# One-hots of a counting sort on Trainium2: bfloat16 digits in pairs from SBUF in place of float32 digits against numbers in PSUM

## What is computed

```python
qkv = x @ qkv_w + qkv_b                              # 12500 x 64 @ 64 x 128
s, t = src, dst
qe = q[s] * 8**-0.5 + (edge_attr @ q_rpe_w + q_rpe_b)
ke = k[t] + (edge_attr @ k_rpe_w + k_rpe_b)
ve = v[t] + (edge_attr @ v_rpe_w + v_rpe_b)
compat = einsum('ehd,ehd->eh', qe, ke)               # 4 heads of 8
ex = exp(compat - segment_max(compat, s)[s])
attn = ex / (segment_sum(ex, s)[s] + 1e-16)
out = segment_sum((ve * attn[..., None]).reshape(e, 64), s)
y = layernorm(x + out)
```

## Time and profile before

| | |
|---|---|
| timed executions | 4825.19 us median (4823.5 to 4829.62) |
| profiled execution, its span | 5645.0 us |
| VectorE busy | 4200.5 us, 74% |
| TensorE busy | 3997.8 us, 71%; weight loads 3559.9 us, 63% |
| GpSimd busy | 3570.5 us, 63% |
| ScalarE busy | 2869.3 us, 51% |
| granted TensorE clock | 0.50 from 282 to 5076 us, 0.97 to 0.99 after |
| DMA engines | 34% to 35% in the sort, 83% to 98% after |

### The profile page before, as it was taken

How to read it: one execution, slowest core, us unless ns; L and a number is a source line. 1 busy time by engine, 2 the same in 40 slices (tenths; PEclk the granted TensorE clock), 3 DMA queues, 4 the chain that set the end, 5 groups by cost and what they waited for, 6 DMA issues and landing times. The chain is left out here.

```text
span 5645.0 us, 94294 instructions
## 1 busy us (share of the span) xinstructions
PE 3997.8 (71%) x18783; PEld 3559.9 (63%) x18783; DVE 4200.5 (74%) x18085; ACT 2869.3 (51%) x6600; POOL 3570.5 (63%) x3772
## 2 busy tenths in 40 slices
PE   7777676777776677677666767777776767748886
PEld 6666666666666666666666666666666666637765
DVE  7777777777777777777777777777777777759998
ACT  3555455555555455455545555555555555524555
POOL 2566666666666666666666666666666666647887
PEclk6555555555555555555555555555555555559999
DMA  6333333333333333333333333333333333369996
GB/s 182 106 110 109 109 107 108 106 107 110 107 111 107 107 110 106 105 111 107 108 107 109 109 110 107 105 112 108 104 110 104 113 108 107 107 159 394 371 356 246
DMA packets 379094, 759.55 MB, mean 135 GB/s; under 512 B 143060, under 2 KB 206875, under 8 KB 365883
## 3 DMA queue, kind: packets, MB, share of 16 engines
q1 hardware_dynamic: 255493, 385.24, 23.1%
q0 software_dynamic: 123520, 373.41, 18.4%
HBM read 570.54 MB, written 187.75 MB: 134 GB/s over the span
## 5 line engine op out<-in xcount | busy, mean ns | idle before, releaser
L634 POOL DMA_INDIRECT rec_dram<-recs,place_i x3223 | 3087.9, 958 | 1819.0 <-issue 1634.2
L670 DVE SCALAR_TENSOR_TENSOR matches<-ids_b,src_f,ps_const 128x128 bf16<-128x128 int16 (+3 forms) x3232 | 1643.9, 543 | 543.5 <-issue 524.0
L786 PE MATMUL ps_feat<-w_in,edge_in 51*128 51x128 f32 x6464 | 1688.5, 438 | 31.9 <-issue 31.4
L769 PE MATMUL ps_look<-free_rec,lo_hotT 128*128 128x98 f32 x6464 | 1609.3, 431 | 1.9 <-ACT lo_hotT L812 1.9
L786 PEld LDWEIGHTS ps_feat<-w_in,edge_in 51*128 51x128 f32 x6464 | 1442.7, 325 | 177.6 <-issue 177.0
L769 PEld LDWEIGHTS ps_look<-free_rec,lo_hotT 128*128 128x128 f32 x6464 | 1473.1, 333 | 2.1 <-ACT lo_hotT L812 2.1
L760 PE MATMUL ps_cnt<-hi_hot,lo_hot 128*128 128x98 bf16 x3232 | 406.0, 276 | 1407.8 <-ACT free_rec L824 787.7
L824 ACT ACTIVATE free_rec<-ps_cnt 128x98 f32<-128x98 f32 x808 | 194.7, 241 | 2366.5 <-remote 2242.4
L760 PEld LDWEIGHTS ps_cnt<-hi_hot,lo_hot 128*128 128x128 bf16 x3232 | 238.3, 127 | 1617.9 <-issue 873.9
L679 DVE CUSTOM_DVE_ANT_0 picked<-hi_hot,ps_look 128x98 f32<-128x98 bf16 x3232 | 652.9, 252 | 123.4 <-issue 114.0
L659 DVE TENSOR_TENSOR lo_hot<-lo_f,ps_const 128x512 bf16<-128x512 bf16 (+1 forms) x808 | 549.9, 681 | 39.0 <-issue 39.0
(11 more groups left out here) (187 smaller groups left out, 2282.0 us busy)
## 6 DMA issues: line engine op xcount, KB each, us to landing
ids_b<-id_dram SPq DMA_DIRECT2D x808, 384.0 KB
rec_dram<-recs,place_i POOLq DMA_INDIRECT x3223
edge_in<-in_attr SPq DMA_DIRECT2D x808, 36.0 KB
w_in<-kv_dram SPq DMA_DIRECT2D x808, 12.0 KB
qx_dram<-qx SPq DMA_DIRECT2D x1, 4753.0 KB
kv_dram<-kvt SPq DMA_DIRECT2D x14, 336.0 KB, 3.7
xt<-in_xT SPq DMA_DIRECT2D x14, 224.0 KB, 3.7
origin<-in_dst_tiles SPq DMA_DIRECT2D x1, 1616.0 KB, 9.3
```

What stands on the lines that cost most here:

```text
L634: pool.indirect_dma_start(rec_dram[:, :], bass.IndirectOffsetOnAxis(place_i[j][:, m:m + 1], 0), recs[j][:, m, 0:ROW], None).then_inc(scatt ...
L670: last = dve.scalar_tensor_tensor(matches[j % NS][:, junk:junk + before], ids_b[j][:, 1, 0:before], src_f[:, bass.ds(u * CT + m, 1)], ps_c ...
L769: last = nc.tensor.matmul(ps_look[j % NS][:, m, 0:NB], lo_hotT[j % NS][:, P * m:P * (m + 1)], free_rec[j % 2][:, :], start=True, stop=True)
L786: last = nc.tensor.matmul(ps_feat[j % 2][:, m, :], edge_in[j][0:K_ROWS, tile], w_in[j][0:K_ROWS, :], start=True, stop=True)
```

## The change

The digits `lo_f` and `hi_f` are stored as bfloat16 in place of float32 (both hold whole numbers up to 127). `lo_hot` and `hi_hot` take the layout of the tables stage: two tiles innermost, [pair of tiles, number, tile of the pair]. The numbers 0 to 127, each twice, stand in a bfloat16 tile `number` in SBUF in place of slice 0 of `ps_const` in PSUM. So both inputs of the two comparisons are bfloat16 in SBUF with two adjacent elements innermost. TensorE's products and VectorE's pick read the one-hots with a step of two elements. One constant's transposition on TensorE goes, and a VectorE cast of 128 x 128 becomes one of 128 x 256. No instruction of the loops is added, removed or moved on any engine; the lines below `number` are one number higher than before (L659 becomes L660).

```diff
-        T["lo_f"] = digits.enter_context(nc.sbuf_tensor("lo_f", [P, NT], F32))
-        T["hi_f"] = digits.enter_context(nc.sbuf_tensor("hi_f", [P, NT], F32))
+        T["lo_f"] = digits.enter_context(nc.sbuf_tensor("lo_f", [P, NT], BF16))
+        T["hi_f"] = digits.enter_context(nc.sbuf_tensor("hi_f", [P, NT], BF16))
...
-        lo_hot = [sb(f"lo_hot{c}", [P, CT, P], BF16) for c in range(NU)]
-        hi_hot = [sb(f"hi_hot{c}", [P, CT, NB], BF16) for c in range(NU)]
+        lo_hot = [sb(f"lo_hot{c}", [P, CT // 2, P, 2], BF16) for c in range(NU)]
+        hi_hot = [sb(f"hi_hot{c}", [P, CT // 2, NB, 2], BF16) for c in range(NU)]
+        number = sb("number", [P, P, 2], BF16)
...
-        number_b = sb("number_b", [P, P], BF16)
...
             def hots(u, j):
                 tiles = bass.ds(u * CT, CT)
-                dve.tensor_tensor(lo_hot[j][:, :, :], lo_f[:, tiles].unsqueeze(2).broadcast_to((P, CT, P)),
-                                  ps_const[:, 0:1, :].broadcast_to((P, CT, P)), ALU.is_equal)
-                dve.tensor_tensor(hi_hot[j][:, :, :], hi_f[:, tiles].unsqueeze(2).broadcast_to((P, CT, NB)),
-                                  ps_const[:, 0:1, 0:NB].broadcast_to((P, CT, NB)), ALU.is_equal).then_inc(hots_made, 1)
+                in_pairs = lambda digit, n: digit[:, tiles].rearrange("p (k a t) -> p k a t", a=1, t=2).broadcast_to((P, CT // 2, n, 2))
+                dve.tensor_tensor(lo_hot[j][:, :, :, :], number[:, :, :].unsqueeze(1).broadcast_to((P, CT // 2, P, 2)),
+                                  in_pairs(lo_f, P), ALU.is_equal)
+                dve.tensor_tensor(hi_hot[j][:, :, :, :], number[:, 0:NB, :].unsqueeze(1).broadcast_to((P, CT // 2, NB, 2)),
+                                  in_pairs(hi_f, NB), ALU.is_equal).then_inc(hots_made, 1)
...
-                    out=picked[j % NS][:, m, :], in0=hi_hot[j][:, m, :], in1=ps_look[j % NS][:, m, 0:NB], scale=1.0, scalar=0.0,
+                    out=picked[j % NS][:, m, :], in0=hi_hot[j][:, m // 2, :, m % 2], in1=ps_look[j % NS][:, m, 0:NB], scale=1.0, scalar=0.0,
...
-                    last = nc.tensor.matmul(ps_cnt[:, 0:NB], lo_hot[j][:, m, :], hi_hot[j][:, m, :], start=False, stop=False,
+                    last = nc.tensor.matmul(ps_cnt[:, 0:NB], lo_hot[j][:, m // 2, :, m % 2], hi_hot[j][:, m // 2, :, m % 2], start=False, stop=False,
...
-            dve.tensor_copy(number_b[:, :], iota_p[:, :].broadcast_to((P, P))).then_inc(const_in, 1)
+            dve.tensor_copy(number[:, :, :], iota_f[:, :].unsqueeze(2).broadcast_to((P, P, 2))).then_inc(const_in, 1)
...
-            for k, turned in enumerate((number_b,) + (ones_b,) * (CT - 1) + (later_b,)):
+            for k, turned in enumerate((ones_b,) * (CT - 1) + (later_b,), 1):
```

## The result

The changed kernel takes 4874.17 us (median of 4 executions, 4867.25 to 4875.71), the kernel before 4827.11 us beside it. The ratio is 1.0097, 95% interval 1.0086 to 1.0109: 47 us slower, where +24 was forecast. The profiled execution spans 4871.2 us, so the long pauses of the profile before are absent, and it can be read against the timed ones.

The account below looks back on a forecast made before the run. GpSimd's scatters were taken to bound the sort. To 4825.2 us came +29 for scatters held back by the one-hots and -5 for the sort's head, giving 4849 us, range 4808 to 4900 us.

Parts of the forecast that it names:

- what bounds the sort: Steady sort: GpSimd's four scatters need 5.04 us a unit, so VectorE's saved 0.453 us a unit counts as nothing.
- the head: First some 12 units of the sort: GpSimd waits on the one-hots, so 0.453 us comes off each, -5.4 us.
- the mechanism: GpSimd's scatters: one starting while VectorE streams two SBUF operands waits; one under way loses nothing; +29 us in all.
- lo_hot's term: Scatters starting behind lo_hot's start are held, up to 242 ns; the working gives 155 hits and 18.8 us.
- arbitrary phase: VectorE against GpSimd in the sort: offset is arbitrary, 33% of units catch a scatter, 36 ns each, +29 us; chance 0.52.
- hi_hot's term: Scatters starting behind hi_hot's start are held, up to 180 ns; sized at 115 hits and 10.4 us.
- rival (1): Sort: scatter starts fall outside both one-hots' holds, only the head counts, 4820 us; chance 0.24.
- (2): Sort: scatter starts are locked into lo_hot's hold, 100 to 242 ns a unit, 4905 to 5016 us; chance 0.08.
- (3): GpSimd's scatters are held at any point, not only at their start: 259 us, 5079 us; chance 0.04.
- (4): GpSimd's queue at records runs dry behind VectorE, whose shorter unit fills that: 4800 to 4815 us; chance 0.10.
- (5): One-hots: pairs don't bring the double rate, holds last 508 and 384 ns, +130 us, 4950 us; chance 0.02.

Follow-up runs that it names:

- the profile taken again: The kernel before, unchanged, run and profiled once more; 4818.38 us, its profile spanning 4816.7 us without pauses.
- 71 hits alone: Kernel before with only lo_hot in the new form, hi_hot's numbers left in PSUM; 4826.98 us, ratio 1.0016.
- ahead of place: Changed kernel with both one-hots moved ahead of place in VectorE's steady step; 4858.15 us, ratio 1.0078.
- behind the picks: Changed kernel with both one-hots moved right behind the next unit's picks on VectorE; 4816.85 us, ratio 0.9992.
- hi_hot from SBUF: Changed kernel with only hi_hot's numbers read from SBUF, lo_hot's pairs from PSUM; 4849.27 us, ratio 1.0045.
- the run of lo_hot: Changed kernel with only lo_hot's numbers read from SBUF, hi_hot's pairs from PSUM; 4826.86 us, ratio 1.0004.
- the single rate: Kernel before with float32 numbers in SBUF: old layout and rate, both comparison inputs in SBUF; 4956.61 us, ratio 1.0285.
- hi_hot alone: Kernel before with only hi_hot in the new form, lo_hot's numbers left in PSUM; 4822.75 us, ratio 1.0010.

## Why the prediction was wrong

**Right: what bounds the sort, and what doesn't count.** GpSimd's scatters bound it. The saved 0.45 us a unit buys nothing in the steady sort, as 0.6 us more costs nothing there. The profile that I had did not show what I wrote of the other engines, though: from 200 to 4900 us its records is never idle, and it starts 28.6 us (median) behind the scatter that it has to wait for. The wait for a landing shows only in the profile taken again (1446.5 us).

**Right: the head.** 6.20 to 5.75 us a unit as forecast; GpSimd's idle time there falls by 20.0 - 13.4 = 6.6 us, against -5.4.

**Right: the mechanism.** A scatter that starts while a comparison streams two SBUF operands waits; scatters under way keep 958 or 959 ns in every variant. The sums of offset and delay are 292 ns for lo_hot and 229 for hi_hot (290 and 230 forecast). One reading was too wide: L691 is not the only operation with two SBUF inputs, L690 (`place_i`) reads `first` and `rank`, of 4 elements each. That changes no term.

**Right by luck: lo_hot's term.** 154 hits and 19.1 us, where the working gives 155 and 18.8. The same working, with the same arbitrary phase, would give them to lo_hot wherever it stands, and lo_hot had 71 hits alone, 92 with hi_hot's numbers in PSUM, 246 ahead of place and 23 behind the picks.

**Wrong: "I take the arbitrary phase, because ACT restarts DVE on a scatter's landing and landings share the DMA engines with 384 KB loads."** It sized hi_hot's term at 115 hits and 10.4 us; it measured 320 and 36.6. Those 26 us are the error. The landings scatter by much less than the 1.26 us between two scatters. After the change records starts 2.25 to 2.8 us behind the start of the last scatter it waits for in 86% of the units, median 2.50. hi_hot follows records by 1.245 us, its hold ends 0.23 us later, and the third scatter of a unit starts 3.79 us behind that same scatter. They meet when records starts 2.31 to 2.52 us behind, which it does in 47% of the units after the change, and in 58% before it (200 to 4200 us). 475 of the 498 long scatters are a unit's third. In the kernel before, records starts 2.41 us behind (median):

```profile
2500.99 0.96 POOL L634 DMA_INDIRECT rec_dram<-recs,place_i  x1 [0.30 <-issue]
...
2502.26 0.96 POOL L634 DMA_INDIRECT rec_dram<-recs,place_i  x1 [0.30 <-issue]
...
2503.33 0.60 ACT L799 ACTIVATE recs<-ps_feat 128x512 f32<-128x512 f32 x1 [1.78 <-DMA rec_dram<-recs,place_i]
2503.52 0.96 POOL L634 DMA_INDIRECT rec_dram<-recs,place_i  x1 [0.30 <-issue]
...
2504.24 0.68 DVE L659 TENSOR_TENSOR lo_hot<-lo_f,ps_const 128x512 bf16<-128x512 bf16 x1
...
2504.79 0.96 POOL L634 DMA_INDIRECT rec_dram<-recs,place_i  x1 [0.30 <-issue]
2504.84 0.56 DVE L661 TENSOR_TENSOR hi_hot<-hi_f,ps_const 128x392 bf16<-128x392 bf16 x1
```

Here records (2503.33) starts 2.34 us behind the scatter at 2500.99, and the third scatter after that one (2504.79) 1.46 us behind records: inside the hold that hi_hot's new place has, 1.265 to 1.474 us behind records.

Had I laid the two new holds, at their new offsets from records, over this profile, it would have given some 430 hits and 30 us for hi_hot, some 120 and 10 us for lo_hot: 40 us of scatters and about +34 with the head. The profile that I did have, with its 852 us of pauses and its records 28.6 us behind, shows nothing of this phase. I held against rival (1) that it isn't in the steady state, and then took from the same doubt that there is no fixed phase at all.

**The rivals.** (1), the phase misses, is what the one-hots behind the picks do, not the changed kernel. (2), the phase hits, came half true: hi_hot, not lo_hot, is the one that is locked, and 4874 us lies under its 4905. (3) fell with the variants' scatters under way unchanged, (4) with a GpSimd that is idle 20 us in all beyond its regular gap, and with 467 us of added work that cost 5.5, (5) with 418 ns.

**Open.** After the change records starts 0.1 us later behind its scatter (2.50 against 2.41), since that scatter lands later (2.43 us behind its start against 2.33, medians). hi_hot's numbers in SBUF are enough for this shift (2.52 in that run), lo_hot's are not (2.42). A later records brings more scatters into lo_hot's hold: laid over the trace of hi_hot from SBUF, it would meet some 180 to 210, against 92 in the run of lo_hot. So the 10 us that lo_hot's hits cost more with both (19.1 against 9.4) may well be this shift. The 10 us more behind hi_hot (36.6 against 26.7) stay open, and so does why a held scatter lands later.

## What to carry to other kernels

Before you speed up a VectorE operation beside a busy GpSimd queue, ask where its inputs lie: with one of them in PSUM a comparison cost the scatters nothing, at the same double rate. When two engines are tied by a semaphore chain, don't average over a phase; measure the offset from the event that restarts the chain, in a profile whose span equals the timed runs. And what a hold costs hangs on its place in the engine's order: the same instructions gave +62, +47, +38 or, within the noise of none, -4 us.

## What the runs showed of the hardware

**The hold has a sharp rule.** Start offset plus delay is constant, to some 10 ns, for each operation, and is its streaming time (1.04 or 0.52 ns an element) plus about 25 ns: 159 = 133 + 26 for qk, 229 = 204 + 25, 292 = 266 + 26, 431 = 408 + 23 and 558 = 533 + 25 for the single rate. Put otherwise, it is the comparison's recorded duration less 125 to 127 ns: 284, 354, 418, 558 and 684 ns in the median. That form also fits rows that the first doesn't: a qk that took 334 ns in the kernel with hi_hot alone has a sum of 209. The double rate nearly halves the hold (292 ns against 558); with one input in PSUM there was none.

**It goes by who is first, with a short tie.** A scatter that starts 20 ns behind hi_hot's start goes through, and hi_hot takes 0.41 us in place of 0.35 (the changed kernel). Over seven of the kernels that read paired numbers from SBUF, a one-hot lengthens when a scatter starts between some 45 ns ahead of it and 35 ns behind it, by up to 0.08 us; from 40 ns behind on it is always the scatter that waits:

```profile
2506.22 0.41 DVE L662 TENSOR_TENSOR hi_hot<-number,hi_f 128x392 bf16<-128x392 bf16 x1
2506.24 0.96 POOL L634 DMA_INDIRECT rec_dram<-recs,place_i  x1 [0.30 <-issue]
```

The Trainium skill, "SBUF — State Buffer", section "SBUF: two separate sides", says that whichever operation starts first has the ports for its whole length and the other blocks. For VectorE's side the trace agrees in that a scatter which comes second is held, for a time that ends 125 ns ahead of the comparison's recorded end. For GpSimd's it differs: lo_hot at 2526.18 starts 0.10 us before the end of a scatter, and, in the kernel with the one-hots behind the picks, both one-hots start inside the scatter that runs from 2501.04 to 2502.00. They keep 0.41 and 0.35 us: a scatter delays only what starts nearly together with it, by 0.06 us in the row above.
